# The seam between encoder layers: maxima filled and turned earlier, a norm's offset on POOL, a store ahead of a weight load

## The reference, cut to what matters

```python
def layer(h, p):
    q, k, v = (split_heads(h @ w + b) for w, b in ((wq, bq_), (wk, bk_), (wv, bv_)))
    scores = jnp.einsum('bhqd,bhkd->bhqk', q, k) * scale
    scores = scores * smask
    a = jax.nn.softmax(scores, axis=-1)
    att = jnp.einsum('bhqk,bhkd->bhqd', a, v)
    att = att.transpose(0, 2, 1, 3).reshape(Bx, Sx, Dx) @ wo + bo_
    h = _ln(h + att, g1, be1)
    ff = jax.nn.gelu(h @ w1 + b1_, approximate=False) @ w2 + b2_
    h = _ln(h + ff, g2, be2)
    return (h, None)
```

## Time and profile before

| | us |
|---|---|
| median of 3 timed runs | 4387.25 |
| lowest and highest | 4385.47, 4394.29 |
| the profiled execution's own time | 4401.41 |
| its span, first to last instruction | 4399.4 |
| TensorE busy | 3681.0 (84% of the span) |
| VectorE busy | 2582.4 (59%) |
| ScalarE busy | 1901.8 (43%) |
| POOL busy | 909.2 (21%) |
| the granted clock of TensorE, mean | 0.905 of full |

### The profile page before, as it was taken

One profiled execution on the slowest core, in us unless ns is written; L12 is line 12 of the kernel. 1 busy time (PEld: TensorE's weight loads), 2 busy tenths in 40 slices (PEclk: granted clock), 3 DMA queues, 4 the chain that ended last, 5 costly groups with the idle time before them and its releaser, 6 DMA issues. The chain is left out here.

```text
span 4399.4 us, 70782 instructions
## 1 busy us (share of the span) xinstructions
PE 3681.0 (84%) x27255; PEld 2539.8 (58%) x27255; DVE 2582.4 (59%) x6589; ACT 1901.8 (43%) x3053; POOL 909.2 (21%) x1164
## 2 busy tenths in 40 slices
PE   5998998998998998985999978677756667997996
PEld 3666666665675666654777745455535433443664
DVE  4866866856857857843222239888668561113663
ACT  2565564564564565553333345232223122331443
POOL 2324333333333332321000001000100230003321
PEclk8998998998998998997999988699867667997997
DMA  5524424524424524401000000000000000003430
GB/s 131 122 47 113 115 50 113 120 52 103 119 60 100 118 56 105 107 20 44 1 1 1 1 15 1 0 1 1 1 6 1 4 1 27 0 0 83 96 86 24
DMA packets 156739, 224.99 MB, mean 51 GB/s; under 512 B 16158, under 2 KB 136350, under 8 KB 139422
## 3 DMA queue, kind: packets, MB, share of 16 engines
q10 hardware_dynamic: 19656, 107.37, 11.2%
q1 hardware_dynamic: 136750, 113.11, 9.4%
HBM read 156.84 MB, written 60.82 MB: 49 GB/s over the span
## 5 line engine op out<-in xcount | busy, mean ns | idle before, releaser
L865 DVE TENSOR_REDUCE enc_mx<-psum 128x2 f32<-128x512 f32 (+1 forms) x1152 | 755.3, 685 | 166.3 <-PE psum L547 162.5
L1032 ACT ACTIVATE enc_e<-psum 128x1024 f32<-128x1024 f32 (+1 forms) x768 | 580.3, 808 | 438.0 <-PE psum L568 313.3
L547 PE MATMUL psum<-enc_ks,enc_qs 80*128 80x128 bf16 (+1 forms) x3072 | 471.5, 259 | 77.5 <-DVE enc_mx L865 64.0
L568 PE MATMUL psum<-enc_qs,enc_ks 83*128 83x256 bf16 (+1 forms) x3072 | 385.9, 251 | 49.8 <-ACT enc_e L1032 35.7
L547 PEld LDWEIGHTS psum<-enc_ks,enc_qs 80*128 80x128 bf16 x3072 | 223.4, 101 | 207.4 <-DVE enc_mx L865 129.7
L579 PE MATMUL psum<-enc_e,enc_v 128*32 128x256 f32 (+1 forms) x6144 | 333.3, 335 | 0.0
L568 PEld LDWEIGHTS psum<-enc_qs,enc_ks 83*128 83x128 bf16 x3072 | 261.9, 99 | 89.2 <-ACT enc_e L1032 45.3
L1913 ACT ACTIVATE moe_act_h<-psum 128x512 f32<-128x512 f32 x288 | 169.2, 598 | 306.1 <-PE psum L1787 305.9
L1809 PEld LDWEIGHTS psum<-par_s,moe_act_h 128*128 128x128 f32 x2304 | 269.7, 192 | 30.1 <-issue 28.5
L1876 DVE SCALAR_TENSOR_TENSOR moe_acc<-psum,moe_gates,moe_acc 128x128 f32<-128x128 f32 x256 | 72.1, 344 | 345.3 <-PE psum L1809 345.3
L1809 PE MATMUL psum<-par_s,moe_act_h 128*128 128x128 f32 x2304 | 272.6, 275 | 0.0
(11 more groups left out here) (483 smaller groups left out, 7072.3 us busy)
## 6 DMA issues: line engine op xcount, KB each, us to landing
enc_qs<-q_pieces ACTq DMA_DIRECT2D x234, 192.0 KB
enc_ks<-k_pieces ACTq DMA_DIRECT2D x234, 192.0 KB
k_pieces<-enc_pieces SPq DMA_DIRECT2D x240, 128.0 KB, 2.0
q_pieces<-enc_pieces SPq DMA_DIRECT2D x144, 128.0 KB, 2.2
enc_qs<-q_pieces SPq DMA_DIRECT2D x54, 192.0 KB
enc_ks<-k_pieces SPq DMA_DIRECT2D x54, 192.0 KB
rope_qs<-q_pieces ACTq DMA_DIRECT2D x39, 192.0 KB
rope_ks<-k_pieces ACTq DMA_DIRECT2D x39, 192.0 KB
```

Source lines behind the costliest of these rows:

```text
L547: last = T_.matmul(p1[f % 2][:, i * kw:(i + 1) * kw], qs[0:KEYED, slot, h, j * P:(j + 1) * P], ks[0:KEYED, slot, h, 0:kw], start=True, sto ...
L568: last = T_.matmul(p2[ch][:, g], ks[0:SCORED, slot, 4 * T + g, ch * P:(ch + 1) * P], qs[0:SCORED, slot, 4 * T + g, 0:n], start=True, stop= ...
L865: V.tensor_reduce(mx[:, u % 2, j * HEADS + h0:j * HEADS + h0 + n], p1[f % 2].rearrange("p (h k) -> p h k", h=n), AX_X, ALU.max)\
L1032: A.activation(e_of(T, ch), p2[ch], ACT.Exp, scale=HD ** -0.5).then_inc(s_e, 1)
```

## The change

Six edits, all in the encoder.

1. Of the fills of sequence 0, six stand in the second product of group 5 and six in that of group 6; six of sequence 1 stand in that of group 7, and six are left after it. VectorE's reductions move with them.
2. The turn of sequence 0's maxima stands in group 7's product, after the fill behind its second tile. POOL's cut of them stands behind the root and offset of group 6; ScalarE's exponential of them (`fall`) and `move_max` stand ahead of its application of group 6's norm.
3. The offset is computed by POOL, right behind the root, from a mean that VectorE has negated beside the variance sum.
4. The last group's turn goes to bank 7 instead of `misc`. The first projection waits for group 6's write-back in place of group 7's; the products with the values wait for group 7's at the third head group.
5. SyncE's store of group 2 goes ahead of the wait for, and the load of, the second set of weights.
6. At the start of the feed-forward part ScalarE copies the last sums before the first GELUs.

```diff
@@ class PairChain @@
+        V.tensor_scalar(self.minus[:, n % 2], self.meanvar[:, n % 2, :, 0], -1.0, None, ALU.mult)
         V.tensor_scalar(self.vareps[:, n % 2], self.meanvar[:, n % 2, :, 1], 1e-5, None, ALU.add).then_inc(self.s_vareps, 1)
-    def centre(self, dve, n):
-        dve.wait_ge(self.s_rstd, n + 1)
-        self.c.nc.vector.scalar_tensor_tensor(out=self.offset[:, n % 2], in0=self.meanvar[:, n % 2, :, 0], scalar=-1.0, in1=self.rstd[:, n % 2],
-                                              op0=ALU.mult, op1=ALU.mult).then_inc(self.s_offset, 1)
+    def centre(self, pool, n):
+        pool.wait_ge(self.s_rstd, n + 1)
+        self.c.nc.gpsimd.tensor_tensor(self.offset[:, n % 2], self.minus[:, n % 2], self.rstd[:, n % 2], ALU.mult).then_inc(self.s_offset, 1)
@@ SyncE, attend @@
+                    if u % 2 == 0 and u // 2 + 2 < GROUPS:
+                        store(layer, 0, u // 2 + 2)
                     if u == 0 and layer:
                         sp.wait_ge(N2.s_done, layer * GROUPS + GROUPS)
                         sp.wait_ge(s_res2, layer * GROUPS + GROUPS)
                         sp.dma_start(LR.sb[:], ...).then_inc(LR.sem, 16)
-                    if u % 2 == 0 and u // 2 + 2 < GROUPS:
-                        store(layer, 0, u // 2 + 2)
@@ POOL, attend @@
                     if g:
                         N2.root(pool, at(layer, GROUPS, g - 1))
+                        N2.centre(pool, at(layer, GROUPS, g - 1))
+                    if g == GROUPS - 1 and not last:
+                        cut_maxima(layer, 1, 0)
...
-                if not last:
-                    cut_maxima(layer, 1, 0)
                 N2.root(pool, at(layer, GROUPS, GROUPS - 1))
+                N2.centre(pool, at(layer, GROUPS, GROUPS - 1))
@@ TensorE @@
                 if u and T % 2 == 0:
                     pe.wait_ge(s_num, at(layer, 32, 2 * u + T // 2 - 1))
+                elif T == 2 and layer:
+                    pe.wait_ge(N2.s_done, at(layer, GROUPS, GROUPS))
...
                             if layer:
-                                last_turn(layer - 1)
+                                pe.wait_ge(N2.s_moved, at(layer - 1, GROUPS, GROUPS))
+                                last_turn(layer - 1, down_bank)
...
                             elif m == 0:
-                                pe.wait_ge(N2.s_done, at(layer, GROUPS, GROUPS))
+                                pe.wait_ge(N2.s_done, at(layer, GROUPS, GROUPS - 1))
...
                 def among(g, t):
-                    if last_layer or g < 6:
+                    if last_layer or g < 5:
                         return
                     for f in range(2) if t < 0 else range(t + 2, t + 3):
-                        fill(layer, 1, 0, 6 * (g - 6) + f)
+                        fill(layer, 1, (g - 5) // 2, 6 * ((g - 5) % 2) + f)
+                    if g == GROUPS - 1 and t == 1:
+                        pe.wait_ge(N2.s_done, at(layer, GROUPS, GROUPS + 6))
+                        turn_max(layer, 1, 0)
...
                 if not last_layer:
-                    for f in range(6):
-                        fill(layer, 1, 1, f)
-                    pe.wait_ge(N2.s_done, at(layer, GROUPS, GROUPS + 6))
-                    turn_max(layer, 1, 0)
                     for f in range(6, 9):
                         fill(layer, 1, 1, f)
                     turn_rows(GROUPS - 2)
                     for f in range(9, 12):
                         fill(layer, 1, 1, f)
@@ VectorE, attend @@
-                    if g >= 6 and go_on:
+                    if g >= 5 and go_on:
                         for f in range(2):
-                            reduce(layer, 1, g // 8, 6 * (g % 2) * (g < 8) + f)
-                    N2.centre(dve, n)
+                            reduce(layer, 1, (g - 5) // 2, 6 * ((g - 5) % 2) + f)
...
-                    if g >= 6 and go_on:
-                        for f in range(2, 12 if g == 8 else 6):
-                            reduce(layer, 1, g // 8, 6 * (g % 2) * (g < 8) + f)
+                    if g >= 5 and go_on:
+                        for f in range(2, 6):
+                            reduce(layer, 1, (g - 5) // 2, 6 * ((g - 5) % 2) + f)
@@ ScalarE, attend @@
+                move_sums(layer, SEQS - 1, 1)
                 gelu(layer, 0)
-                move_sums(layer, SEQS - 1, 1)
...
                     if g >= 2 and not last:
-                        back2(layer, g - 2)
+                        back2(layer, g - 2, misc)
+                    if g == GROUPS - 1 and not last:
+                        fall(layer, 1, 0)
+                        move_max(layer, 1, 0)
                     if g:
                         apply2(layer, g - 1, last)
...
                 else:
-                    fall(layer, 1, 0)
+                    back2(layer, GROUPS - 2, misc)
                     apply2(layer, GROUPS - 1, False)
-                    move_max(layer, 1, 0)
-                    back2(layer, GROUPS - 2)
```

More of the change, by code:

```diff
@@ L672, in close, with last_turn @@
                     N4.turn(pe, g, bank[1])
-            def last_turn(layer):
-                pe.wait_ge(N2.s_done, at(layer, GROUPS, 2 * GROUPS - 1))
-                N2.turn(pe, at(layer, GROUPS, GROUPS - 1), misc)
+            def last_turn(layer, b):
+                N2.turn(pe, at(layer, GROUPS, GROUPS - 1), b)
             def attend(layer, last_layer):
@@ L811, in attend @@
                 if last_layer:
-                    last_turn(layer)
+                    pe.wait_ge(N2.s_done, at(layer, GROUPS, 2 * GROUPS - 1))
+                    last_turn(layer, misc)
                     for k in range(GROUPS, GROUPS + 5):
@@ L1056, in apply2, with back2 @@
                 N2.apply(act, n)
-            def back2(layer, g):
-                N2.back(act, at(layer, GROUPS, g), misc, grp(g), LR["g2"], LR["be2"])
+            def back2(layer, g, b):
+                N2.back(act, at(layer, GROUPS, g), b, grp(g), LR["g2"], LR["be2"])
             def close(k):
@@ L1119, in attend @@
                     if g and last:
-                        back2(layer, g - 1)
+                        back2(layer, g - 1, misc)
                     if g in (2, 3) and not last:
@@ L1129, in attend @@
                     apply2(layer, GROUPS - 1, True)
-                    back2(layer, GROUPS - 1)
+                    back2(layer, GROUPS - 1, misc)
                     for k in range(GROUPS, GROUPS + 5):
```

4 lines of the change are left out of this document (2 added, 2 removed).

## The result

The changed kernel takes 4342.94 us at the median of four runs (4332.21 to 4348.48), the kernel before, run beside it, 4390.77. The ratio is 0.9884, with a 95% interval of 0.9855 to 0.9913: about 51 us faster. The forecast was 4325, the range 4304 to 4347. The interval of the ratio stands for a gain of 38 to 64 us, so the times alone don't tell the forecast's 62 from the measured 51. The profiled execution took 4348.48 us; it is the slowest of the four. Single executions in experiments 7 and 11 took 7226 and 13323 us; they are left out of the ratios, and the times of these two experiments are medians of the other three.

What follows compares the result with a forecast made beforehand. Waits at five seams, and a slow clock behind them, were taken as the bound. Per seam 1.2 + 3.3 + 5.0 + 7.4 - 2.5 = 14.4 us; 73 at full clock, 51 at low; falls at half: 62, so 4325 us, range 4304 to 4347.

Steps and rivals of the forecast that it cites:

- What bounds the kernel, and the sign: At five seams between encoder layers TensorE pays for waits, then for a slow clock behind them; the change makes it faster.
- Feed-forward start: Copying the last sums before the GELUs saves TensorE's wait: 1.2 us, six times, between 0.6 and 1.27.
- Fills and tail: Moving fills into groups 5 to 7 brings the first scores earlier: 3.3 us a seam, between 0.5 and 5.
- rival (e): Slower: group 5's fill waits for sequence 0's load, with TensorE behind it; 4405 at 16 us late; chance 0.03.
- Offset on POOL: The offset behind POOL's root costs 0.3 us, between 0.1 and 1.0; VectorE's added negation costs 0.1.
- rival (c): VectorE bounds groups 5 and 6; with a held negation and slow offset 2 us per seam go: 4346; chance 0.07.
- Last turn and sequence 0: Sequence 0 at the seam lasts 15.1 us instead of 20.1: gain 5.0 at full clock, some 4.5 lost at low.
- Third store: Store ahead of the weights: sequence 1 gains 7.4 us, between 5.5 and 8, less 2.5 for the load late next.
- rival (b): The clock falls at every seam, as before: 51 us gained, 4336; chance 0.18.
- (a): The clock holds at every seam: 4314, or 4301 with the load in time too; chance 0.18.
- (d): The store stays late behind the row of maxima in SyncE's queue; sequence 1's 7.4 us not gained: 4350; chance 0.06.

Runs made afterwards that it cites:

- experiment 7: Changed kernel with the second weights' load one sequence later and 6 and 12 unread transposes in the tail's waits: 4311.86 us, ratio 0.9817.
- experiment 11: The kernel of experiment 10 with the last group's turn back in misc (edit 4 undone): 4305.05 us, ratio 0.9789.
- experiment 5: Changed kernel with the offset back on VectorE and without the negation (edit 3 undone): 4340.19 us, ratio 0.9882.
- experiment 2: Changed kernel with unread transposes on TensorE, 6 ahead of group 7's third fill and 12 ahead of the third fill behind it: 4318.48 us, ratio 0.9827.
- experiment 10: Changed kernel with second weights' load one sequence later, group 2's queries stored first, and 7, 16 and 8 unread transposes: 4301.00 us, ratio 0.9782.
- experiment 1: Changed kernel with the load of the second weights one sequence later, behind sequence 2's row of maxima: 4327.01 us, ratio 0.9849.
- experiment 3: Changed kernel with the store of group 2 behind the weights again: 4365.75 us, ratio 0.9935.
- experiment 4: Changed kernel with four of VectorE's last six reductions ahead of the last group's statistics: 4342.07 us, ratio 0.9882.
- experiment 9: Changed kernel with the second weights' load one sequence later and group 2's queries stored first, no unread transposes: 4320.47 us, ratio 0.9830.
- experiment 12: Changed kernel with ScalarE's load of sequence 4 moved behind the move of sequence 2's row of maxima: 4361.00 us, ratio 0.9914.

## Why the prediction was right in kind and 18 us too low

**What bounds the kernel, and the sign.** Right. The seams paid for waits and for the clock behind them, and both became less.

**Feed-forward start.** 1.2 us taken, 1.5 measured (from `up` to `up`, 5.46 to 3.97 us), above the upper end of 1.27: the wait of 1.27 counts from the end of the `up` before, and without it the turn also overlaps that end by 0.16 us (3.54 from start to start, for a stretch of 3.70). The GELUs' delay didn't reach TensorE.

**Fills and tail.** 3.3 us taken; 3.0 measured, as the whole stretch from the feed-forward start is 4.5 us shorter and 1.5 of it is the start's. In the fifth seam, where the clock stayed full until 0.5 us before the scores, it is 3.7: the sum had no term for a fall ahead of the first scores. The waits foreseen at 1.3, 0.9 and one long stretch of 2.7 us are there, at 1.03, 0.52 and 2.39. No fill of group 5 waits for sequence 0's load, so rival (e) fell. The row of maxima's landing is hidden.

**Offset on POOL.** Its price of 0.3 us was close:

```profile
L231 POOL TENSOR_TENSOR enc_n_offset<-enc_n_minus,enc_n_rstd x48: 198/201/204, 313.2 to 1945.6; 128x4 f32<-128x4 f32 x48
L222 DVE TENSOR_SCALAR enc_n_minus<-enc_n_meanvar x48: 169/170/172, 311.8 to 1944.2; 128x4 f32<-128x4 f32 x48
```

The negation is held in none of 48 cases, and rival (c) fell. But I had read the 48 equal rows of the variance sum as speaking against the rule in the Trainium skill's "SBUF — State Buffer", section "Who interferes with whom", and that reading was wrong: in the traces no operation of POOL runs beside any of the 48 variance sums before, or beside any of the 48 negations after. POOL's root waits for the variance sum, and POOL stands idle then. These rows test the rule in neither direction. The old centring did have POOL beside it, in 36 of 48 cases. Experiment 5 adds what I had not foreseen: by time the edit as a whole can't be told from nothing here, and at a full clock it is worth 0.7 us a seam.

**Last turn and sequence 0. This is the step that failed:** "My forecast is a fall at about half of the seams." The clock fell in all five. At full clock the step was right, even low: 15.1 us foreseen, 14.3 measured (experiments 2 and 10), which is 5.3 us below the old mean of 19.6. But a fall costs 5.1 us when it covers two thirds of the sequence (clock 0.66, three seams) and 2.2 when it covers one third (0.83, two seams), 3.9 on average; I had taken 4.5 at half of the seams, 2.25. Of 5.3 us only 1.4 were left. How long a fall lasts is partly chance: these five are from the slowest execution, and sequence 0's mean in the other kernels without unread work that end the tail alike is up to 1.2 us less (experiment 1). That it falls is not: in the profiles of the changed kernel and experiments 1, 3, 4, 5, 9 and 12 the granted clock of sequence 0 was 0.66 to 0.88 in all 35 seams. I argued that idle time in pieces makes the fall less sure. With the pieces of 1.03 and 2.39 us mostly filled the clock was 1.00 in three seams of five, and with more of them filled in all five (experiments 10 and 11). The argument that I had cited for the other side, that the old kernel's clock fell behind a gap of only 2.56 us, was the one to follow.

**Third store.** 7.4 us less 2.5 taken, 4.9 a seam; 4.7 measured between the kernels, 4.6 by experiment 3. Both terms were too small, and their errors nearly cancel, which is luck: without any wait sequence 1 lasts 12.4 us (12.7 foreseen), 8.0 less than the old mean of 20.4, and what is late next costs 3.3 us on average (15.7 less 12.4), 1.8 to 2.9 of it a wait at the start of sequence 2 in four seams. That place was right. The releaser is not the load itself but a row of 24 KB that it holds and that lands with it (experiment 12). The weights cost the load something too: from its first issue to its last packet it takes 10.7 us on average in the changed kernel and 8.7 in experiment 1, and its first packet moves 2.4 to 2.6 us after the issue instead of 0.9. That is 1.9 us for the overlap that I had put at 2.6. The Trainium skill's "DMA: Bandwidth & Descriptors", section "Queues, rings and completion order", adds that an engine finishes a whole packet of one queue before it turns to the next. I had applied that to the load against the weights only; it speaks of the row against the load as well. That the row's packets start later beside the load agrees with it, though no run here changes the size of a packet.

**What was missing.** A fall of the clock behind the new wait: sequence 2 lost 0.7 us on average, where I had counted none.

In sum: 4.5 + 1.4 + 4.7 - 0.7 = 9.9 us a seam, the value of rival (b), the clock falling at every seam. Its 4336 was 51 us below the old median, and the ratio gives 51. The median came out at 4343 for two reasons: a fourth execution moved the old median up by 3.5 us, and the rest is the spread of single executions. So of the 18 us, 11 are the forecast's own (62 against 51): 7 by the falls in sequence 0, 3.5 by those in sequence 2, the rest by small terms of both signs. Rivals (a), (c), (d) and (e) fell.

## What to carry to other kernels

Where a kernel stands still and then runs at a low clock, cost the waits and the clock as two terms, and don't count on short waits to keep the clock up: it fell behind 1.03, 0.52, 0.57 and 2.39 us as it had behind 2.56 and 1.37, and cost up to 5 us in each of five seams. It stayed full in every seam only where the waits had been filled with work, down to 0.65 us at the longest in the tail (experiments 10 and 11). Ask of every small transfer on the path what large one is under way when it is issued, whichever queue that is in. And measure an edit that shortens one stretch together with the next: of 1.8 us saved in the tail by reordering reductions, sequence 0 took back 2.3 at the same clock. Where the clock falls for a longer or shorter time from one execution to the next, don't credit an edit with a gain in a stretch ahead of it, as would have happened with 4.5 of experiment 1's 11 us.

## What the runs showed of the hardware that was not expected

Work that nothing reads makes the kernel faster: 18 transposes in each of five seams, in time in which TensorE waited, took 24 us off by the medians and 19 in the seams of the profiles, with the granted clock of sequence 0 at 0.89 to 1.00 instead of 0.66 to 0.83. And a DMA of 24 KB took 5.0 us to its use while a load of six DMAs of 192 KB moved on the other engine's queue, and 2.95 us without it or with only its last 2 us left.
